# Pair products of a recommender tower: from SBUF through DRAM to SBUF, or from SBUF to SBUF directly

## What is computed

```python
e = jnp.stack([tbl_0[ids[:, 0]], ..., tbl_26[ids[:, 26]]], axis=1)
interactions = jnp.einsum('bnd,bmd->bnm', e, e)
i, j = jnp.triu_indices(27, k=1)
z = interactions[:, i, j]
h = jnp.concatenate([z, dense_ctx], axis=1)
h = jnp.maximum(h @ W_top1 + b_top1, 0.0)
h = jnp.maximum(h @ W_top2 + b_top2, 0.0)
y = h @ W_top3
```

## Time and profile before

| what | value |
|---|---|
| time, three runs | 168.25, 169.30, 169.31 us |
| span of the profiled execution | 166.6 us |
| mean granted TensorE clock | 0.867 |
| TensorE busy (matmul) | 119.2 us, 72% |
| POOL busy (gathers) | 78.1 us, 47% |
| bytes moved | 16.45 MB; HBM written 1.71 MB |
| zT from pair_blocks and pair_tail | 16 transfers, about 60 KB and 52 KB each |

### The profile page before, as it was taken

The page is one execution under the profiler, slowest core; times in us unless marked ns, Lnnn a source line. Parts: engine busy times, 40 slices in busy tenths (PEclk is TensorE's granted clock), DMA queues, the critical chain, the costliest instruction groups (busy, mean ns, idle before and its releaser), DMA issues.

```text
span 166.6 us, 1949 instructions
## 1 busy us (share of the span) xinstructions
PE 119.2 (72%) x712; PEld 103.3 (62%) x712; DVE 66.6 (40%) x135; ACT 65.0 (39%) x107; POOL 78.1 (47%) x80
## 2 busy tenths in 40 slices
PE   6439949376357095870798997442399999999995
PEld 6437728255245083650677996441299999799993
DVE  3537539372520553770304650200071464346221
ACT  3050948555490553621904650210062263245110
POOL 2377777777777687887800077777200000000000
PEclk9975999999978969699579999655558999999999
DMA  2344444444445466994300036122115003300600
GB/s 47 117 165 145 158 156 159 160 157 156 155 160 162 152 125 161 208 204 148 95 16 4 0 112 142 47 63 51 31 45 115 0 4 102 57 0 29 134 0 4
DMA packets 15751, 16.45 MB, mean 99 GB/s; under 512 B 10099, under 2 KB 12211, under 8 KB 15614
## 3 DMA queue, kind: packets, MB, share of 16 engines
q1 hardware_dynamic: 13308, 11.35, 22.6%
q0 software_dynamic: 2304, 4.72, 11.6%
q10 hardware_dynamic: 130, 0.26, 0.6%
HBM read 14.62 MB, written 1.71 MB: 98 GB/s over the span
## 4 chain that ended last, share of the span: by engine, by line
PE 51%; issue 19%; DMA 12%; another core or an unknown queue 7%; ACT 5%; DVE 4%; SPq 1%; DVEq 0%; ACTq 0%
PE psG L319 18%; PE psG L302 12%; DMA table<-in_tbl 12%; PE psH L333 8%; PE psH L363 5%; PE psT L282 4%; DVE hot L416 3%; PE psG L345 2%; ACT ET L483 1%; PE psH L376 1%; ACT parts L495 1%; ACT hot L502 1%; ACT hot L506 1%; DVE parts L421 1%
## 5 line engine op out<-in xcount | busy, mean ns | idle before, releaser
L269 POOL DMA_INDIRECT rows<-in_tbl,ids_sb x72 | 77.2, 1072 | 38.8 <-issue 21.0
L302 PE MATMUL psG<-hot,parts 125*128 125x512 f32 x156 | 47.7, 470 | 31.3 <-issue 13.9
L302 PEld LDWEIGHTS psG<-hot,parts 125*128 125x128 f32 x156 | 35.8, 235 | 42.1 <-issue 28.5
L319 PE MATMUL psG<-ET 128*122 128x104 f32 x256 | 31.7, 279 | 7.6 <-issue 6.8
L319 PEld LDWEIGHTS psG<-ET 128*122 128x122 f32 x256 | 30.1, 194 | 8.4 <-issue 8.3
L416 DVE TENSOR_SCALAR hot<-pick_ids,row_no 125x512 fp32r<-125x512 int32 x65 | 26.7, 482 | 19.8 <-remote 11.3
L431 DVE COPY gram<-psG 26x208 f32<-26x208 f32 (+1 forms) x17 | 8.2, 485 | 31.9 <-remote 14.5
L523 ACT COPY gram<-psG 26x208 f32<-26x208 f32 (+1 forms) x17 | 8.3, 489 | 31.2 <-PE psG L319 14.3
L421 DVE TENSOR_TENSOR parts<-table,parts 125x1024 fp32r<-125x1024 f32 (+1 forms) x9 | 11.8, 1313 | 20.8 <-ACT parts L495 18.2
L483 ACT COPY ET<-psG 128x512 f32<-128x512 f32 x9 | 9.8, 1085 | 19.1 <-remote 10.4
L495 ACT CAST parts<-table 125x1024 fp32r<-125x1024 f32 (+1 forms) x8 | 9.0, 1128 | 17.5 <-DMA table<-in_tbl 17.5
(11 more groups left out here) (27 smaller groups left out, 45.3 us busy)
## 6 DMA issues: line engine op xcount, KB each, us to landing
table<-in_tbl SPq DMA_DIRECT2D x6, 500.0 KB
pick_ids<-in_picked_ids SPq DMA_DIRECT2D x8, 250.0 KB
table<-in_tbl SPq DMA_DIRECT2D x3, 625.0 KB
pair_blocks<-gram SPq DMA_DIRECT2D x8, 176.0 KB, 1.9
rows<-in_tbl,ids_sb POOLq DMA_INDIRECT x72
w_sb<-in_w SPq DMA_DIRECT2D x1, 1024.0 KB
zT<-pair_blocks SPq DMA_DIRECT2D x12, 60.5 KB
w_sb<-in_w SPq DMA_DIRECT2D x1, 512.0 KB
```

The costliest lines, as they stand in the source:

```text
L269: pool.indirect_dma_start(out=rows[:, t % 2, f, :], out_offset=None, in_=gathered_tables[f], in_offset=bass.IndirectOffsetOnAxis(ap=ids_sb ...
L302: last = pe.matmul(psP[:, k % 2, :], parts[:, k % 2, x, c, :], hot[:, k % 2, c, :], start=x == 0 and c == 0, stop=x == 1 and c == CH[k] - 1)
L319: last = pe.matmul(o, stationary, group[:, :, 1:F], start=True, stop=True)
```

## The change

The two DRAM tensors and their semaphores go. SP no longer writes gram to DRAM and reads it back; it issues, for each chunk, four transfers from gram straight into zT, one for each group of 32 samples. All four count up the same chunk_in, so whoever waits for a chunk waits for 64 in place of 16. The copies into a gram buffer that is used again wait for the four chunks of tile t-2, in place of the three writes.

```diff
-            def read_rows(t, c, block, i0, ni, w):
-                src = block.rearrange("(s i) (j g) -> s i j g", s=S, g=G)[:, i0:i0 + ni, :, :].rearrange(
-                    "s i j g -> (i j) s g")
-                sp.dma_start(zT[0:ni * w, t, c, :].rearrange("r (s g) -> r s g", s=S), src
-                             ).then_inc(chunk_in[t][c], 16)
+            def move_pairs(t, c, i0, ni, j0, w):
+                for s in range(S):
+                    sp.dma_start(zT[0:ni * w, t, c, G * s:G * (s + 1)],
+                                 gram[Q * s + i0:Q * s + i0 + ni, t % 2, j0:j0 + w, :]).then_inc(chunk_in[t][c], 16)
 
             for t in range(T):
                 sp.wait_ge(gram_dve, U * (t + 1))
                 sp.wait_ge(gram_act, U * (t + 1))
-                for b in range(2):
-                    sp.dma_start(blocks[t, b], gram[:, t % 2, W * b:W * (b + 1), :].rearrange("p j g -> p (j g)")
-                                 ).then_inc(blocks_out[t][b], 16)
-                sp.dma_start(tail[t], gram[:, t % 2, 2 * W:J, :].rearrange("p j g -> p (j g)")
-                             ).then_inc(tail_out[t], 16)
-                sp.wait_ge(blocks_out[t][0], 16)
-                read_rows(t, 0, blocks[t, 0], 0, W, W)
-                sp.wait_ge(blocks_out[t][1], 16)
-                read_rows(t, 1, blocks[t, 1], 0, W, W)
-                read_rows(t, 2, blocks[t, 1], W, W, W)
-                sp.wait_ge(tail_out[t], 16)
-                read_rows(t, 3, tail[t], 0, J, TAIL)
+                move_pairs(t, 0, 0, W, 0, W)
+                move_pairs(t, 1, 0, W, W, W)
+                move_pairs(t, 2, W, W, W, W)
+                move_pairs(t, 3, 0, J, 2 * W, TAIL)
...
-                    pe.wait_ge(chunk_in[t][c], 16)
+                    pe.wait_ge(chunk_in[t][c], 16 * S)
...
                 if m // U >= 2:
-                    dve.wait_ge(blocks_out[m // U - 2][0], 16)
-                    dve.wait_ge(blocks_out[m // U - 2][1], 16)
-                    dve.wait_ge(tail_out[m // U - 2], 16)
+                    for c in range(NC):
+                        dve.wait_ge(chunk_in[m // U - 2][c], 16 * S)
```

More of the change, by code:

```diff
@@ L102, in dlrm_tower @@
         psP = psG[:, :, 0, :]
-        blocks = nc.dram_tensor("pair_blocks", (T, 2, P, W * G), fp32, kind="Internal").ap()
-        tail = nc.dram_tensor("pair_tail", (T, P, TAIL * G), fp32, kind="Internal").ap()
         ids_in = sem("ids_in")
@@ L134, in dlrm_tower @@
         gram_act = sem("gram_act")
-        blocks_out = [[sem(f"blocks_out_{t}_{b}") for b in range(2)] for t in range(T)]
-        tail_out = [sem(f"tail_out_{t}") for t in range(T)]
         chunk_in = [[sem(f"chunk_in_{t}_{c}") for c in range(NC)] for t in range(T)]
@@ L342, in last_layer1 @@
                     pe.wait_ge(gram_act, U * T)
-                pe.wait_ge(chunk_in[T - 1][c], 16)
+                pe.wait_ge(chunk_in[T - 1][c], 16 * S)
                 for n in ORDER:
@@ L517, in unit_copies @@
                 if m // U >= 2:
-                    act.wait_ge(blocks_out[m // U - 2][0], 16)
-                    act.wait_ge(blocks_out[m // U - 2][1], 16)
-                    act.wait_ge(tail_out[m // U - 2], 16)
+                    for c in range(NC):
+                        act.wait_ge(chunk_in[m // U - 2][c], 16 * S)
                 for x, banks in enumerate(UNIT_BANKS[m]):
```

## The result

The changed kernel takes 184.24 us (median of four runs, 183.62 to 184.81), the kernel before 169.31 on the same chip: a ratio of 1.093, 95% interval 1.087 to 1.099. It is slower by 15 us, where 0.9 were forecast.

The account below looks back on a forecast made before the run. TensorE's own work was taken to bound the end from 120 us; 0.9 us for tile 3's late chunk 3, added to 169.3, gave 170.2 us, range 168.0 to 172.5.

Parts of the forecast that it names:

- What bounds the kernel: From 120 us TensorE's own list of work sets the end; the detour through DRAM costs nothing.
- The pitch: SP's queue, time from issue to issue: 0.38 us for the first, 0.50 for the others; bounds 0.39 and 0.70.
- my own formula: Tile 3, chunk 3: lateness 14p - 6.2 us for p from issue to issue, beginning at p = 0.44.
- The landing: Issue to landing of a new SBUF to SBUF transfer: 1.4 us, bounds 1.3 and 2.0.
- The other tiles: Tiles 0 to 2: issues and landing take 8.8 us against 22.1, 14.4 and 12.9 of room, so they fit.
- the hole: TensorE's idle stretch, 103 to 120 us: held for a matter of gathers and TensorE, which the change leaves alone.
- Tile 3, the mechanism: Tile 3: SP's 16 issues bring chunk 3 0.8 us late, 0.9 with the release; the work behind moves with it.
- SP becomes the bound: Rival, chunk 3 of tile 3: pitch 0.55 to 0.70 or landing 2.0 us, giving 170.8 to 172.9 us; chance 0.20.
- The rival: Idle stretch 103 to 120 us moves: closes in part, 161 to 166 us, chance 0.12; grows 2 us or more, 0.04.
- HBM traffic: 1.7 MB written and as much read goes away; no row shows anyone waiting for it.

Follow-up runs that it names:

- the bursts: Kernel before plus nine bursts of six SP transfers after the result; 0.64 to 0.88 us an issue between SBUF sides, 0.38 to 0.48 with a DRAM side.
- tile 3 alone: Kernel before with only tile 3 moved from SBUF to SBUF, tiles 0 to 2 through DRAM; 179.63 against 169.76 us, ratio 1.061.
- form 6: Burst of six SBUF to SBUF transfers, 16 partitions x 1,024 bytes to 128 x 128, added behind the kernel before; 0.64 us an issue.

## Why the prediction was wrong

- **What bounds the kernel: right.** TensorE's list sets the end from 120 us on, and the old detour was covered: in the profile before no wait of TensorE names a transfer of pairs.
- **The pitch: the step that failed.** I took 0.50 us from the read of the same tile and bounded it at 0.70 by the load into zT. Measured: 0.87. All my rows had a DRAM side, and I reasoned that the cost hardly depends on what is moved, which the bursts bear out for pieces and bytes but not for where the two sides lie. No row bore on that, and the upper bound should have stood further off; the loads right behind rows 7, at up to 4.32 us an issue, could have warned me. By my own formula the lateness at tile 3 is 14 x 0.87 - 6.2 = 6.0 us.
- **The landing: too short.** 1.4 us taken, 2.03 measured, just outside my bound of 2.0: 0.6 us more. The formula also took 0.38 for the first step, which was 0.87: 0.5 more, 7.1 together. That is what tile 3 alone shows: its chunk 3 starts 16.19 us after tile 2's first layer, against 9.09 before. In the changed kernel it is 5.95 and not 7.1, because there tile 2's first layer itself waits, and SP starts 1.2 us earlier beside it.
- **The clock: a missing term.** From the start of chunk 3 to the end are 7.72 us in place of 5.62. These 2.1 us, at half clock after the waits, make up the rest of the 8.1.
- **The other tiles: wrong by the same number.** "8.8 us, against 22.1, 14.4 and 12.9" becomes 15 us from first issue to last landing, which fits tile 0 alone: tiles 1 and 2 wait 1.49 and 0.97 us. That tile 0 fits was itself a gift of the hole.
- **Tile 3, the mechanism: right**, as the forecast and the rival "SP becomes the bound" had it; only its size was off, and its price ended at 172.9 us where 184.2 came.
- **The hole: half right.** It is a matter of gathers and TensorE, as argued from the earlier trace rows: holding the pair transfers left it, leaving out gathers removed it there. But the change does not leave it alone: 5.6 us. The rival gave 0.04 to its growing by 2 us or more.
- **HBM traffic: right**, nobody waited for it; written bytes fell to 0.00 MB.

**What stays open:** by what the hole becomes longer. Four profiles with tile 0 going from SBUF to SBUF have it end 5.9 to 6.1 us after the last gather, and four with tile 0 through DRAM 3.2 to 3.5 us after it; whether that is the form of the transfers or their number was not told, since the kernels made for it met only chips without the hole. With other matmuls beside the gathers the late signal came 2.7 and 5.3 us after the last of them, with no pair transfer at all, so the distance is no fixed number either. Nor is it known why the hole is on some chips only. Whether 16 engines or another shape gave the 0.64 us of form 6, and so a cheaper cut of the direct transfers, was not tried. None of the kernels run is clearly faster than the one before on a chip without the hole.

## What to carry to other kernels

Count issues on the queue, not only bytes: sixteen transfers of 15 KB cost 14 us of SP's time here, where seven larger ones and three waits cost 3.7. When a profile holds no transfer whose two sides both lie where the new ones would, leave the price open upwards, or measure a burst of it first. And before removing a detour, look whether anyone waits for it: here nobody did.

## What the runs showed of the hardware

In bursts of six, a transfer with both sides in SBUF cost SP 0.79 to 0.88 us to issue with 11, 44 or 121 partitions, and 0.64 with 16 to 128; with one side in DRAM 0.38 to 0.48, though behind a load of 1 MB an issue took up to 4.32 us. From issue to landing were 2.0 us from SBUF to SBUF and 1.4 to DRAM, for the same 11 pieces of 1,408 bytes. POOL issued eight of the direct transfers in 4.7 us, where SP took 6.9. The same kernel took 169 us on some chips and 146 on others: on the first, TensorE's signals came up to 18 us late in the kernel before, and 23 in the changed one, while POOL issued gathers, and on the second they did not. Comparisons hold within one chip only.
